# Edge stage of a graph kernel: the second layer's 24 products taken by channel block and part over four tiles

## The reference

```python
ei = jnp.concatenate([x[src], edge_attr], axis=-1)      # 256 + 64 channels
core = jnp.maximum(ei @ W1 + b1, 0.0) @ W2 + b2         # the second layer: @ W2
gate = jax.nn.sigmoid(ei @ Wg + bg)
msg = gate * core
agg = jax.ops.segment_sum(msg, dst, num_segments=x.shape[0])
out = agg + x
```

## Time and profile before

| | |
|---|---|
| median of 3 runs | 2689.19 us |
| span of the profiled execution | 2722.1 us |
| TensorE busy over the span | 2389.6 us (88%) |
| VectorE busy | 2076.2 us (76%) |
| ScalarE busy | 1493.1 us (55%) |
| GpSimd busy | 1663.0 us (61%) |
| products of `core_product` | 157.5 to 1636.8 us |

### The profile page before, as it was taken

The page is one execution under the profiler, slowest core; times in us unless marked ns, Lnnn a source line. Parts: engine busy times, 40 slices in busy tenths (PEclk is TensorE's granted clock), DMA queues, the critical chain, the costliest instruction groups (busy, mean ns, idle before and its releaser), DMA issues.

```text
span 2722.1 us, 50965 instructions
## 1 busy us (share of the span) xinstructions
PE 2389.6 (88%) x16049; PEld 1845.0 (68%) x16049; DVE 2076.2 (76%) x4860; ACT 1493.1 (55%) x2727; POOL 1663.0 (61%) x1581
## 2 busy tenths in 40 slices
PE   7879999999999999999899894689888899888864
PEld 3479999999999998888889881245444444444443
DVE  6658888888889888888889998897777763436455
ACT  1157777777767776676767674454665640112123
POOL 0367777777677776667667661456555645666663
PEclk9989999999999999999999996899999999998976
DMA  6555555555555555555555542254455425665542
GB/s 210 207 154 158 161 167 160 161 163 164 157 160 164 165 157 161 164 170 169 164 163 165 161 143 83 80 138 126 119 142 140 126 92 189 209 228 162 188 129 88
DMA packets 276289, 422.45 MB, mean 155 GB/s; under 512 B 127634, under 2 KB 198692, under 8 KB 274004
## 3 DMA queue, kind: packets, MB, share of 16 engines
q0 software_dynamic: 90368, 281.11, 34.6%
q1 hardware_dynamic: 170028, 116.99, 14.3%
q10 hardware_dynamic: 15656, 21.30, 2.3%
HBM read 354.91 MB, written 64.37 MB: 154 GB/s over the span
## 4 chain that ended last, share of the span: by engine, by line
PE 53%; DVE 18%; issue 9%; ACT 8%; another core or an unknown queue 7%; DMA 2%; DVEq 1%; POOL 1%; ACTq 1%; SPq 0%; POOLq 0%
PE banks L972 15%; PE banks L1060 5%; PE banks L949 5%; PE banks L1034 4%; PE banks L1086 3%; PE banks L856 3%; ACT counts L1432 2%; PE banks L1102 2%; PE banks L946 2%; DVE hidden_lo L1767 2%; PE banks L947 2%; ACT hidden_hi L1296 2%; DVE room L1786 2%; PE banks L960 2%
## 5 line engine op out<-in xcount | busy, mean ns | idle before, releaser
L797 POOL DMA_INDIRECT gathered<-p_table,src_t x784 | 807.2, 1030 | 439.7 <-DVE gate L1778 252.8
L797 POOL DMA_INDIRECT gathered<-hop_table,src_t x576 | 585.5, 1017 | 463.1 <-PE banks L1102 174.8
L972 PE MATMUL banks<-w_hi,hidden_hi 128*128 128x256 f32 x1568 | 462.1, 295 | 55.1 <-DVE hidden_lo L1767 48.6
L972 PE MATMUL banks<-w_lo,hidden_hi 128*128 128x256 f32 x1568 | 443.6, 283 | 0.0
L972 PE MATMUL banks<-w_hi,hidden_lo 128*128 128x256 f32 x1568 | 443.5, 283 | 0.0
L1432 ACT CAST counts<-banks 128x686 f32 (+3 forms) x382 | 295.4, 773 | 213.8 <-PE banks L1037 103.8
L1303 ACT CAST msg_hi<-room 128x512 fp32r<-128x512 f32 x392 | 241.8, 617 | 246.4 <-DVE room L1786 209.5
L1767 DVE SCALAR_TENSOR_TENSOR hidden_lo<-banks,hidden_hi 128x512 fp32r<-128x512 f32 x392 | 270.1, 690 | 121.8 <-ACT hidden_hi L1296 68.4
L972 PEld LDWEIGHTS banks<-w_hi,hidden_hi 128*128 128x128 f32 x1568 | 299.6, 191 | 79.0 <-DVE hidden_lo L1767 66.5
L1034 PE MATMUL banks<-codes,low_hot 128*128 128x343 f16 (+3 forms) x958 | 242.2, 337 | 111.2 <-DVE codes L2002 54.6
L1317 ACT ACTIVATE gate<-gate 128x512 f32<-128x512 f32 x392 | 242.3, 632 | 123.0 <-DVE gate L1778 107.1
(11 more groups left out here) (225 smaller groups left out, 5280.3 us busy)
## 6 DMA issues: line engine op xcount, KB each, us to landing
ea<-in_edge_attr SPq DMA_DIRECT2D x196, 128.0 KB
counts_saved<-counts SPq DMA_DIRECT2D x16, 1568.0 KB
ring<-counts_saved SPq DMA_DIRECT2D x16, 1568.0 KB
gathered<-p_table,src_t POOLq DMA_INDIRECT x784
p_table<-p_t ACTq DMA_DIRECT2D x48, 256.0 KB, 4.1
hop_table<-parts SPq DMA_DIRECT2D x12, 896.0 KB
gathered<-hop_table,src_t POOLq DMA_INDIRECT x576
x_saved<-x_room SPq DMA_DIRECT2D x7, 896.0 KB
```

The source lines that it names most:

```text
L797: pool.indirect_dma_start(out=rows[:, n % slots, j, :], out_offset=None, in_=table[:, :], in_offset=bass.IndirectOffsetOnAxis(ap=src_t[:, ...
L972: last = nc.tensor.matmul(banks[:, 4 + half, j % 2 * H:(j % 2 + 1) * H], lhs, rhs, start=False, stop=n == len(products) - 1, skip_group_ch ...
```

## The change

The products of `core_product` are the same 24, in another order. Before, one wait for both blocks of `hidden_lo` stood ahead of them, and they ran tile by tile. Now the channel block is the outer loop, the part (hi by w_hi, hi by w_lo, lo by w_hi) the next, and the four tiles the innermost. Each block waits for `hidden_upper` ahead of its first part and for `hidden_ready` ahead of its third. Since the first four products go to both banks, the two waits for `core_seeded` both stand ahead of the first. Both raises of `core_done` lie within the last part.

```diff
-                pe.wait_ge(S["hidden_ready"], KC * (g + 1))
                 for half in range(2):
                     pe.wait_ge(S["core_seeded"], 2 * g + half + 1)
-                    for j in range(2 * half, 2 * half + 2):
-                        products = [(a[:, k, j * P:(j + 1) * P], b[:, k, :]) for k in range(KC)
-                                    for a, b in ((hidden_hi, w_2_hi), (hidden_hi, w_2_lo), (hidden_lo, w_2_hi))]
-                        for n, (lhs, rhs) in enumerate(products):
-                            last = nc.tensor.matmul(banks[:, 4 + half, j % 2 * H:(j % 2 + 1) * H], lhs, rhs,
-                                                    start=False, stop=n == len(products) - 1, skip_group_check=True)
-                    last.then_inc(S["core_done"], 1)
+                for k in range(KC):
+                    for n, (lhs, rhs) in enumerate(((hidden_hi, w_2_hi), (hidden_hi, w_2_lo), (hidden_lo, w_2_hi))):
+                        if n == 0:
+                            pe.wait_ge(S["hidden_upper"], KC * g + k + 1)
+                        if n == 2:
+                            pe.wait_ge(S["hidden_ready"], KC * g + k + 1)
+                        final = k == KC - 1 and n == 2
+                        for j in range(TILES):
+                            last = nc.tensor.matmul(banks[:, 4 + j // 2, j % 2 * H:(j % 2 + 1) * H],
+                                                    lhs[:, k, j * P:(j + 1) * P], rhs[:, k, :],
+                                                    start=False, stop=final, skip_group_check=True)
+                            if final and j % 2:
+                                last.then_inc(S["core_done"], 1)
```

## The result

The changed kernel takes 2711.16 us (median of 4 runs, 2708.47 to 2715.26), the kernel before, run beside it, 2691.31 us (4 runs, 2689.13 to 2701.16). The ratio is 1.0063 with a 95% interval of 1.0043 to 1.0083: 0.4 to 0.8% slower. It is slower, by some 9 to 22 us.

A forecast was written before the change was run, and what follows sets the result against it. TensorE was taken to bound the first part of the edge stage, with VectorE close behind in the second. Terms +8.6 + 5.7 + 2 - 0.5 = +15.8 us gave 2705 us, range 2689 to 2724 (forecast's own 2695 to 2724).

The forecast's parts named there:

- The mechanism: Head of the 24 products: the start now needs the second seed, 0.27 us behind `hidden_lo`, delaying TensorE's later work.
- first stretch: First part of the edge stage: 32 waiting groups each lose 0.27 us and the loss adds up, +8.6 us.
- A waiting group's delay: Start of the products: 0.27 us later wherever VectorE is on time, at 606.45 instead of 606.18.
- a met wait costs 0: TensorE's products: a wait already met adds nothing, as the 13th product came 0.12 us behind its neighbour.
- Later stretch: Second part of the edge stage: VectorE's queue absorbs some shifts; half of 43 waits taken, 21 x 0.27 = 5.7 us.
- `core_done`: First bank's raise moves from 12th to 22nd product, VectorE's message waits 0.19 us; estimated 2 us, bounds 0 and 14.
- The gain of the removed wait: Groups where VectorE's own queue makes `hidden_lo` late start earlier; two found, -1.5 us at most, -0.5 taken.
- the 66.6 us: TensorE's waits ahead of the products over both stretches, the whole amount at stake: 2.5% of the time.
- Seeds in time: Rival: late line 949 signals belong to the profiled execution, TensorE's 0.19 us in hand absorbs the shift; 2689 to 2694, chance 0.30.
- the 33 us: Profiled execution's excess over the timed runs, taken as support for late line 949 signals belonging to that execution.
- The removed wait is worth it: Rival: `hidden_lo` mostly ends later than the seeds, so its removal gains some 30 us; 2659 us, chance 0.10.
- The late first half of the message decides: Rival: VectorE idles 0.19 us for bank 4 in some 110 second-stretch groups, 21 us more; 2726 us, chance 0.08.

The follow-up runs named there:

- Bank outermost: Changed kernel's split waits and order within a bank, but all bank 4 products first, each bank behind its own seed: 1.0005 and 0.9963 against the kernel before.
- one wait: Changed kernel with a single wait at the head, for both seeds, and no waits for `hidden_upper`: 2564.89 us, 0.9985 against the kernel before.
- short seeds and all waits: Changed kernel with each seed copy cut to 64 of 512 columns: 2570.76 us, 1.0012 against the kernel before.
- control: The kernel before, run and traced once more with no edit: 2697.76 us, ratio 1.0004; trace span 2691.6 us.

## Why the prediction came out as it did

**The mechanism held.** The first product waits for the second seed, which ends behind `hidden_lo`, and all 24 wait with it. The rows name line 1315 in 41 + 61 = 102 waits, where 70 or more were forecast; the run with only the seed's wait moved shows that it suffices (1.0104). The median of 2711.16 us lies in the forecast's own range, 6 us above its 2705; the loss was forecast at 15.8 us, and the three ratios make it 13 to 17 us at their middle. That the size agrees so well is partly luck. By parts, 8.6 us were forecast for the first stretch and 13.7 measured, and 7.2 for all the rest (5.7 + 2 - 0.5), where about 0.5 was measured: two errors of some 5 and 7 us that nearly cancel.

**A waiting group's delay: 0.27 us forecast, 0.32 measured.** The 0.27 is the distance from `hidden_lo` to the second seed, and that was right (618.59 less 618.31 is 0.28). The start then came 0.10 us behind the release and not 0.05. The step that failed is "a met wait costs 0", which I had read from the 13th product, in the middle of running work. At the head, behind a stopped queue, the start was 0.05 us behind its release before the change, 0.10 with the changed kernel's three waits and 0.14 with three waits in the old order. With two of the three taken away it was 0.05 again, behind the same seed. So the waits there are the cause, though all but the last had long been met. Whether it is their number isn't shown: the orders with 0.10 and 0.14 are also the only ones that wait twice for `core_seeded` at the head.

**First stretch: +8.6 us forecast, +13.7 measured.** Two parts. Each wait is 0.32 us longer, which makes 32 x 0.32 = 10.2 us. And there are 41 waits where there were 32: I had counted a loss of 0 wherever TensorE didn't wait before, with 0.19 us in hand. With the start 0.32 us later that reserve is gone in groups that lie near it. Nine more waits of at most 0.32 us are 2.9 us. Together 13.1 of the 18.2 us by which the products' wait grew; the rest stays open, since how late the signals behind line 949 come differs from group to group in both traces.

**Later stretch: +5.7 forecast, +0.5 measured.** The products' wait there grew by 14.2 us, more than I gave it, and the stage didn't get that much longer: 11.8 us less is waited at lines 946 and 986, and the clock was at its lower level for less time. The forecast had the sign of the effect (part is absorbed), but not its place, VectorE's reserve. Why TensorE waits less at line 946 isn't settled: the profile names no releaser for those waits ("issue").

**`core_done`: 2 us forecast, nothing clear of noise.** VectorE's small waits came as said (11.9 us in 49 times, 4.4 in 16). A late raise alone gives 1.0006 [0.9994, 1.0019], which leaves room for the 2 us. The Trainium skill (page Perfetto Trace Analysis, section Matmuls) would have independent groups rotate through PSUM banks so that one's evacuation lies beside the next's matmuls. What it protects, an early evacuation of bank 4, was worth nothing that could be measured here. Bank outermost with the parts' waits still wins on the third chip, 0.4 to 0.8% against the kernel before, for the other reason that its start needs neither the second bank's seed nor `hidden_lo`.

**The gain of the removed wait: -0.5 us.** I had found two groups in which the start could come ahead of `hidden_lo`; in the trace after there are three. Where only the first seed is wanted at the head, the same removal gives -0.4 to -0.8% on the third chip. So the opportunity in the 66.6 us was real; the change closed it in the act. This is the part of my working that I would do otherwise: I asked what the removed wait is worth in this order, and not whether the second condition could be kept off the head.

**The rivals.** *Seeds in time*: its mechanism exists. On the second chip TensorE is bound by its own 7.01 us in the first stretch, and the second seed's wait costs nothing (0.9985 [0.9976, 0.9994] with one wait; 1.0012 [1.0003, 1.0020] with short seeds and all waits). My condition for it was wrong: I asked whether the late signal belongs to the profiled execution. The control, at 2691.6 us as short as the timed runs, has its 32 waits in the first stretch as well, so the 33 us weren't that lateness. The late signal was there in every set but that of the second chip, and in none of the four traces of that one; that it goes with the chip is what this suggests, not more. The changed kernel itself, with full seeds and all its waits, was not run on that chip, so its own ratio there stays open. *The removed wait is worth it*: false for this change, true of bank outermost on the third chip. *The late first half of the message decides*: it would have cost 20 us and more in the second stretch, where +0.5 was measured; and the seed's wait alone, with `core_done` as before, has the whole loss.

## What to carry to other kernels

Before a wait is taken off the head of a queue, look which condition ends second, and whether the new order pulls it forward too: here a wait worth up to 66 us was exchanged for one that ended 0.28 us later. Arrange the order so that the first instructions need only what is ready first (one bank, one seed), even if later ones then come in an order that looks less even. An engine's late operation can't simply be put earlier in its queue: first add up the chain behind what it displaces, since 1.1 us there cost 3.7% of the time.

## What the runs showed of the hardware

**The same kernel, another chip, other signals.** The kernel before took 2568.44 us on one chip and 2696.64 and 2731.09 on two others, some 5 to 6% apart, with a spread of some 0.4 to 0.7% within each set. In the edge stage the difference is in the time from the end of the last transposes to ScalarE's start: 0.31 us in the group shown of the one (ScalarE came from its own work, so the signal took no longer), 1.76 us in that of the control on another; the trace ahead of the prediction has 1.40 (618.13 to 619.53). It isn't so in every group: in the first stretch ScalarE sat idle ahead of the second `hidden_hi` in 34 groups of the control and 37 of the changed kernel, and in one group in each of the four traces of the second chip. That stage ends 37 us apart (last products at 1587 and at 1625 us), so most of the difference lies behind it, and I haven't traced it there. What makes a signal late isn't shown, and since the second chip had one set of runs, the chip can't be told from the occasion there.

**Long stops of TensorE without a named releaser, and the clock behind them.** In the control, TensorE stopped for 3.11 us ahead of line 946, and the profile names nothing that it waited for:

```profile
1025.29 0.77 PE L946 MATMUL banks<-ea_turned_sb,w_e_hi 128*128 128x512 f32 x1 [3.11 <-issue]
```

The stretch before it and that which follows, by engine, with the granted clock behind POOL's count:

```profile
1018.00:1025.00 7.00, 3.77 (x30) 3.32 (x28) 5.89 (x11) 3.91 (x8) 4.86 (x5) 0.95 0.86 294
1025.00:1031.00 6.00, 5.71 (x23) 5.14 (x24) 1.98 (x5) 2.70 (x5) 2.89 (x3) 0.50 0.49 138
```

In single microseconds the granted clock is 1.00 up to 1024 us, 0.62 on average from there to 1025, and 0.50, the 1.2 GHz level, behind that: it fell within the stop, before the next product started. A product of line 946 takes 0.77 us where it takes 0.40 at full clock. So the stop is paid a second time: by an estimate from the 0.40 for 0.77, the 6 us behind it hold work for some 3 us at full clock. A shorter stop can do the same: in the changed kernel one of 2.25 us, ahead of the products at 1422.63, was followed by a granted clock of 0.50 from 1424 to 1426 us.

**Waits that are met still show at a stopped head.** The first product starts 0.05 us behind its releaser with one or two waits ahead of it, and 0.10 or 0.14 with three. There is more that this doesn't explain. Bank outermost went from 0.9963 [0.9948, 0.9978] to 0.9916 [0.9892, 0.9940] when two waits a group were taken away that were always met. The two traces start their products at the same distance behind `hidden_hi` (0.54 us), and their stages end within 1 us of each other; their own times, 2709.20 and 2706.51 us, differ by only 0.1%, so they can't show what the 0.5% is made of. What both quicker kernels without the extra waits have in common (this one, and the one with one wait at the head, 0.9985) is 196 recorded instructions fewer, 50769 for 50965, one a group: a wait for a semaphore that stood ahead of the first product by itself. That this is worth 0.2 to 0.5% is a guess that no run here isolates.
